# Row gathers of a graph layer that also wait for a matrix engine's progress

## What is computed

```python
def gat_conv(x, W, attn_l, attn_r, src, dst, n_nodes):
    ...
    e = jax.nn.leaky_relu(el[src] + er[dst], NEG_SLOPE)
    m = jax.ops.segment_max(e, dst, num_segments=n_nodes)
    ex = jnp.exp(e - m[dst])
    denom = jax.ops.segment_sum(ex, dst, num_segments=n_nodes)
    alpha = ex / denom[dst]
    out = jax.ops.segment_sum(alpha[:, :, None] * feat[src], dst, num_segments=n_nodes)
...
    h = jnp.einsum('bfd,edh->bfeh', x, W1) + b1      # all 8 experts
    h = jax.nn.relu(_bn(h, g1, be1, m1, v1))
    h = jnp.einsum('bfeh,ehk->bfek', h, W2) + b2
    h = jax.nn.relu(_bn(h, g2, be2, m2, v2))
    y = jnp.einsum('bfeh,ehd->bfed', h, Wo) + bo
    return jnp.einsum('bfed,fe->bfd', y, w)
```

## Time and profile before

| | us |
|---|---|
| median of 3 runs | 3248.05 (3245.86 to 3252.17) |
| profiled execution, span from first to last instruction | 3526.7 |
| PE busy in it | 2158.3 (61%) |
| DVE busy | 2302.8 (65%) |
| ACT busy | 1906.1 (54%) |
| POOL busy | 2134.4 (61%) |
| mean granted TensorE clock | 0.747 |

### The profile page before, as it was taken

The page is one execution under the profiler, slowest core; times in us unless marked ns, Lnnn a source line. Parts: engine busy times, 40 slices in busy tenths (PEclk is TensorE's granted clock), DMA queues, the critical chain, the costliest instruction groups (busy, mean ns, idle before and its releaser), DMA issues. The chain is left out here.

```text
span 3526.7 us, 33756 instructions
## 1 busy us (share of the span) xinstructions
PE 2158.3 (61%) x7294; PEld 1353.6 (38%) x7294; DVE 2302.8 (65%) x5558; ACT 1906.1 (54%) x6229; POOL 2134.4 (61%) x2028
## 2 busy tenths in 40 slices
PE   6700455555544454544581006888898888888999
PEld 5600333333333332333361003544454444554565
DVE  7882788888988888888563235655466554665631
ACT  3300778787867667766462224544455444554532
POOL 3337677777767777764475666666666666666200
PEclk9855566666755555555796557989898998989999
DMA  6413899999989999998544465555565555555310
GB/s 230 122 21 103 312 338 345 341 348 337 374 330 364 369 345 358 364 348 318 156 127 116 151 226 186 163 167 177 177 190 160 171 173 174 188 171 169 136 33 12
DMA packets 244661, 783.82 MB, mean 222 GB/s; under 512 B 70282, under 2 KB 118253, under 8 KB 217801
## 3 DMA queue, kind: packets, MB, share of 16 engines
q0 software_dynamic: 127664, 369.53, 33.2%
q1 hardware_dynamic: 86715, 391.15, 29.1%
q10 hardware_dynamic: 30078, 20.99, 2.4%
HBM read 404.26 MB, written 378.13 MB: 222 GB/s over the span
## 5 line engine op out<-in xcount | busy, mean ns | idle before, releaser
L1514 POOL DMA_INDIRECT e_rows<-scratch_table,k_src x1664 | 1742.9, 1047 | 816.0 <-issue 400.3
L1624 DVE SCALAR_TENSOR_TENSOR e_ring<-e_ring,k_same,e_rows 128x520 f32<-128x520 f32 (+1 forms) x1560 | 967.6, 620 | 505.0 <-ACT e_rows L1647 179.0
L1647 ACT ACTIVATE e_rows<-e_rows 128x64 f32<-128x64 f32 (+1 forms) x4160 | 1196.9, 371 | 36.4 <-issue 24.9
L2251 PE MATMUL e_p_y<-e_wfo,e_h 128*121 128x256 f32 x1664 | 418.3, 407 | 116.4 <-DVE e_y L2013 67.6
L2251 PEld LDWEIGHTS e_p_y<-e_wfo,e_h 128*121 128x121 f32 x1664 | 325.8, 198 | 224.9 <-issue 128.5
L2225 PE MATMUL e_p_a<-e_xt,e_wf 128*128 128x484 f32 x832 | 387.4, 611 | 10.2 <-ACT e_h L2160 6.5
L2160 ACT ACTIVATE e_h<-e_p_a,e_shift,e_scale 128x484 f32<-128x484 f32 x208 | 151.9, 749 | 435.0 <-remote 282.5
L2237 PE MATMUL e_p_b<-e_h,e_wf 128*128 128x484 f32 x832 | 362.6, 578 | 13.8 <-ACT e_h L2160 11.5
L2013 DVE SCALAR_TENSOR_TENSOR e_y<-e_p_y,e_w,e_y 121x256 f32<-121x256 f32 x416 | 181.0, 476 | 248.5 <-PE e_p_y L2251 101.1
L1017 PE MATMUL e_p_kv<-e_wkv,nd_feat 128*121 128x512 f32 x208 | 190.0, 1066 | 107.2 <-DVE nd_feat L922 73.5
L1593 DVE TENSOR_TENSOR e_rows<-e_rows,e_shared 128x4096 f32<-128x4096 f32 x52 | 229.7, 4416 | 22.5 <-issue 8.9
(11 more groups left out here) (438 smaller groups left out, 3569.4 us busy)
## 6 DMA issues: line engine op xcount, KB each, us to landing
scratch_rows_a<-e_ring SPq DMA_DIRECT2D x104, 2112.0 KB
scratch_sums<-e_ring SPq DMA_DIRECT2D x104, 1032.0 KB
e_rows<-scratch_table,k_src POOLq DMA_INDIRECT x1664
scratch_table<-na_frow ACTq DMA_DIRECT2D x52, 245.8 KB
scratch_table<-hi_frow ACTq DMA_DIRECT2D x52, 124.8 KB
na_x<-in_x SPq DMA_DIRECT2D x13, 484.0 KB
e_wkv<-in_x SPq DMA_DIRECT2D x52, 121.0 KB
scratch_res<-e_wkv SPq DMA_DIRECT2D x52, 121.0 KB
```

The lines of the kernel that those rows point to most:

```text
L1514: nc.gpsimd.indirect_dma_start(out=rows[:, n % B, g, :], out_offset=None, in_=table, in_offset=bass.IndirectOffsetOnAxis(ap=k.src[:, n * G ...
L1624: nc.vector.scalar_tensor_tensor(ring[:, i, j - c0, 0:W + H], prev, k.same[:, n * G + j:n * G + j + 1], rows[:, rb, j, 0:W + H], ALU.mult, ...
L1647: last = nc.scalar.activation(rows[:, rb, j, at], rows[:, rb, j, at], ACT.Copy, scale=rows[:, rb, j, W + h:W + h + 1])
L2251: last = nc.tensor.matmul(self.p_y[bank][0:BK, i * D:(i + 1) * D], self.h2[:, e % 2, kt, v:v + BK], self.wfo[:, e, kt, :], start=kt == 0, ...
```

## The change

POOL gets two more waits in each batch of layer two, both on `y_filled`. `taken(m, second)` gives the count at which both banks of the expert are filled that DVE adds in batch m, at j = 1 and 2 or (`second`) at j = 8 and 9; it gives 0, which means no wait, where there is no such expert yet. Behind the row gather of (n, 0) POOL waits for the expert that DVE adds at (n-2, 8); behind that of (n, 8) for the one that it adds at (n-1, 1). Both are about 24 steps behind the next row gather.

```diff
+    def taken(self, m, second):
+        r, kq = m // PB, m % PB
+        f, e = (r - 2, 2 * kq - 2) if kq else (r - 3, E - 2)
+        return 2 * (f * E + e + (1 if second else 0) + 1) if self.valid(f) else 0
+
     def pool(self, pool, n, j):
+        if j == 0 and n >= 2:
+            wait(pool, self.y_filled, self.taken(n - 2, True))
+        if j == 8 and n >= 1:
+            wait(pool, self.y_filled, self.taken(n - 1, False))
         if n % PB == 0 and n >= 2 * PB and j < 2 * KB:
             self.gather(pool, n // PB - 2, j // 2, j % 2)
```

## The result

| | before | after |
|---|---|---|
| median of 4 runs, side by side, us | 3250.11 (3245.86 to 3253.97) | 3445.98 (3445.87 to 3448.45) |
| ratio | | 1.0605 (95%: 1.059 to 1.062) |
| span of the profiled execution | 3526.7 | 3444.1 |

Slower by 196 us. The forecast was 3335, 87 us more than before, with an upper end of 3445: the sign was right, the size too small by 111 us, and the time lies 1 us above the range. The profiled span fell while the timed median rose, which the prediction had named as the sign that the late signals of the earlier trace rows belonged to the profiler; runs 1 and 2 narrow this to one profiled execution of before. The profiled span after is that of the timed runs.

The account below looks back on a forecast made before the run. Layer two's middle was taken as bound by PE, ACT and DVE waiting for each other. Ten groups going from 102.0 to 109.7 us, plus 10 for the last, gave +87 on 3248, so 3335 us; range 3230 to 3445.

Parts of the forecast that it names:

- late signals: Layer two's middle: PE's signals reach other engines late, most around group gathers; ACT stands 294.3 us in 58 such waits.
- Fill of expert 3 to `below`: Each group: 19.7 us of POOL's gathers plus 3.0 of landing before DVE's first step on the group rows, together 22.7.
- PE's stall: Before expert 5's second layer, PE idles 25.6 - 5.2 = 20.4 us a group, waiting for the bank `keep` frees.
- In proportion: Timed group before the change: 110.7 us scaled by median over profiled span, 0.921, giving 102.0, between 92.0 and 110.7.
- Rival (b): Larger loss: signals are late only under the profiler and a timed group is POOL's 92 us; 3435 us, chance 0.2.
- the tail's 85.4 us: PE's work per group without gathers beside it, taken from after the last gather as base of the group after.
- half a stall: Last group gathered behind a wait, g = 11: its wait is for an earlier expert, so 10 us was taken.
- What bounds the kernel now: Layer two's middle: no engine full, a loop of PE, ACT and DVE waiting for each other, 110.7 us a group.
- The part on row gathers: Waits ahead of row gathers cost DVE nothing; the cover is PE's 10 us per expert, matching eight gathers (10.0 us).
- (a): Faster: timed runs have late signals too and POOL's pauses let them through; 3233 us, or 3188; chance 0.18.
- (c): No change in time: the waits are already met when POOL comes to them; chance 0.04.
- (d): POOL becomes the bound, since eight gathers take as long as PE's expert; 3400 us at worst, chance 0.08.

Follow-up runs that it names:

- run 1: The kernel before, unchanged, profiled a second time; 3241.74 us (one run), profiled span 3239.9.
- run 2: The kernel before, unchanged, profiled a third time; 3247.15 us (one run), profiled span 3245.3.
- run 5: The changed kernel, all waits kept, with the eight group gathers issued one behind another at the released wait; 3348.23 us, ratio 1.0314.
- run 6: The changed kernel with each POOL wait put one expert earlier; 3337.06 us, ratio 1.0285.
- run 7: The changed kernel with each POOL wait put two experts earlier; 3246.94 us, ratio 1.0001.
- run 10: The kernel before with two extra POOL memsets of a spare tile in each batch of layer two; 3340.09 us, ratio 1.0274.
- run 8: The changed kernel, all waits kept, with the group gathers issued a batch earlier, one behind another; 3228.32 us, ratio 0.9946.
- run 4: The changed kernel without the wait ahead of the group gathers, the other seven of a group kept; 3445.67 us, ratio 1.0613.
- run 11: The changed kernel with two extra POOL memsets of a spare tile in each batch; 3510.36 us, ratio 1.0798.

## Why the prediction was right in sign and short in size

**The mechanism held, term by term.** Fill of expert 3 to `below`: 22.7 predicted, 22.35 in the timeline above. Of it the landing was taken as 3.0; from the end of the last issue to `below` it is 2.6. The Trainium skill ("DMA: Bandwidth & Descriptors", section "Anatomy of one DMA — SWDGE (gpsimd) path") has about 2.0 us of fixed cost for a transfer on this path. The measured value lies between the skill's figure and the row's 3.0, and no verdict hangs on it. PE's stall: 20.4 predicted, 19.1 measured, on the line named (second layer of expert 5). Runs 5 to 7 confirm it as a dose: shorten the arrival by 9 or 10 us and the group shortens by as much, and by 20 and the loss is gone.

**The step that failed** is "In proportion (3248.05/3526.7 = 0.921) it is 102.0; I take this since it is between the two and favours neither". The timed group of before is 94.0 (runs 1 and 2, whose spans are the timed runs'). That one term is 10 x 8.0 = 80 of the 111 us. Rival (b), at 0.2, had the right mechanism: 92.0 for the group, and late signals that the timed runs don't have. Its "only under the profiler" is half of it, since two of the three profiled executions don't have them either. The objection raised to it, that the time ahead of layer two may hold all of the excess, does not stand. The first gather of layer two starts at 1884.1 in the first profile of before and at 1811.1 in the second: 73 of the 287 us between the two spans lie ahead of it, and 198 more between the first and the last gather of layer two (3280.3 - 1884.1 for 3008.8 - 1811.1).

**The rest of the miss** is the group after: 109.7 predicted, 113.2 measured. PE's work was taken as the tail's 85.4 us, with 2.4 for the lower clock behind the stall. It is 90.2, at a granted clock of 0.89. The second profile of before has 88.5 (796.17/9, at 0.97), so 3.1 us are there without the change, and the base taken from the tail was too short; what the change adds is 1.7, so the clock was priced 0.7 too high. PE's waits for DVE's additions are 3.9, for the 1.5 that I kept of the gate's waits, which are gone (35.5 us over nine groups, above; in the second profile of before they are there too, 46.4 us in 18). The stall's -1.3 goes the other way. Sum: +3.1 - 0.7 + 2.4 - 1.3 = 3.5, times ten is 35.

**The full account** compares the two undisturbed profiles, after against the second one of before, by the starts of `below`. To g = 0: +3.4. From there to g = 1: +8.8. Nine groups: 1019.0 - 846.3 = +172.7. To g = 11: 104.3 for 83.6, +20.7, where I had half a stall, 10. To g = 12: -1.5. Together 204.1, and the spans differ by 3444.1 - 3239.9 = 204.2. (The timed difference is 196, since this execution of before, 3241.74, lies 8 us under the median of 3250.11.) Two errors of the sum offset each other here, and that is luck: the first of the ten groups grew by 8.8 and not by the 19.2 of the others, `below` having waited 20.23 us at g = 1 before the change already, and the step to g = 11 by 20.7 and not by 10.

**"What bounds the kernel now" was wrong** for the same reason. The middle is not a loop of PE, ACT and DVE that wait for each other; that was the disturbed execution, and that late signals come with gathers does not hold either, since the undisturbed ones have the same gathers and none. It is POOL at 94.0 us, 2 us above the floor that the prediction worked out for it, and run 10 shows it by doing. The part on row gathers, costed at nothing for DVE, holds only with the group gathers elsewhere: in run 8, with the same waits, POOL's longest pause put down to PE is 0.3 us and nothing is lost. With the group gathers in their place it does not hold. Its cover, PE's own pace equal to eight gathers, is what makes POOL unable to come back to its lead, so that run 4's waits alone make the whole stall. The sum has no error from this, since the two sets of waits cost the same stall once.

**The other rivals.** (a) needed a timed group of over 110 us; there is none, and the undisturbed executions have no late signals that pauses could let through. (c) is out by the timeline. (d), POOL as the bound of the changed kernel, would have slowed it by the whole 101 us in run 11; it slowed by 64, by way of a later stall. (d) was right for the kernel before, where I had not looked for it.

## What to carry to other kernels

When the profiled span is far from the timed median, do not split the difference: ask which sum of work explains the median (here POOL's issue, 92.0 us a group, nearly did), and distrust the waits that no work explains. POOL issues its transfers in the order of its code, so a throttle on the bulk transfers also holds the few urgent ones behind it: choose its distance by what is needed first (runs 5 to 8). And where producer and consumer have equal pace, a lead that is lost is not won back (run 4), so taking out the one wait ahead of the urgent transfers does not help.

## What was unexpected of the hardware

One of three profiled executions of the same kernel was 8.9% longer than another (3526.7 against 3239.9), with signals of PE seen up to 19.9 us late by ACT and its gathers on POOL stretched by waits that the others don't have (up to 5.3 us from g = 1 to 10, for 0.3). What delays them there is open: no run made it come back. A POOL memset between two gathers took none of the usual 0.30 us pause of its own (101 us of work, 0.0 idle before it).
